# A graph network with experts: twelve-head outputs kept in SBUF in place, and a fourth block in ten formed by VectorE from two broadcast rows

## The chip, the core and the metric

The kernel runs on one core of a Trainium2 chip. The metric is the device time of one execution in microseconds (us). The runs of the kernel before gave 3488.45, 3494.69 and 3496.25 us.

## What is computed

Four blocks, each with a residual, over 1250 nodes with 768 features: a three-layer graph attention network (heads 12 x 64, 12 x 64, 1 x 768) on 20,000 edges; a mixture of 8 experts, top 2; a two-layer graph attention network (4 x 512, 1 x 768); a second mixture of experts. The change touches the first two attention layers, called layers 0 and 1 below, and the border behind each. One such layer:

```python
def _gat_layer(x, W, attn_l, attn_r, bias, src, dst, num_heads, head_dim, use_elu):
    z = (x @ W).reshape(N, num_heads, head_dim)
    el = jnp.sum(z * attn_l, axis=-1)
    er = jnp.sum(z * attn_r, axis=-1)
    e = jax.nn.leaky_relu(el[src] + er[dst], NEG_SLOPE)      # slope 0.2
    m = jax.ops.segment_max(e, dst, num_segments=N)
    ex = jnp.exp(e - m[dst])
    denom = jax.ops.segment_sum(ex, dst, num_segments=N)
    alpha = ex / denom[dst]
    msg = alpha[:, :, None] * z[src]
    out = jax.ops.segment_sum(msg, dst, num_segments=N)
    out = out + z + bias.reshape(1, num_heads, head_dim)
    if use_elu:
        out = jax.nn.elu(out)
```

## The kernel before

**Dense attention.** The graph is turned once into a dense table of edge counts, source by destination, in SBUF. Nodes are cut into T = 10 tiles of P = 125. A head works on 20 blocks j: two halves of the destinations (HALF = 625 columns) times ten tiles s of sources. A block holds the weights of 125 sources for 625 destinations.

**One block.** With r1 = er - m and r2 = 0.2 er - m per destination, and el per source, the exponent is 0.2 el + max(0.8 el + r1, r2), which is also 0.2 el + relu(0.8 el + 0.8 er) + r2. In layers 0 and 1 the kernel uses the second form:

- ScalarE writes the rectified block, relu(0.8 er + 0.8 el), into `r2[half][:, s % 3]` (`relu`, L1309), three blocks ahead, from a broadcast row of er (`erb`). It does this for all 20 blocks.
- Adding r2, in one of two ways. For most blocks TensorE multiplies by `spread`, an identity with a row of ones below; the row of r2 lies in partition 125 of the same buffer (`exponents`, L1020, two products per block). For the tiles in `ADD_AT` = [3, 7, 9], 6 of the 20 blocks, VectorE adds a broadcast row `rb2` (`add_r2`, L1758) three blocks ahead.
- ScalarE takes the exponential (L1322); VectorE limits it and multiplies by the edge counts into the weights (`weights`, L1681).
- TensorE multiplies the weights of the other half, one half behind, with z and a column of ones (`sum_tile`, L1030). Each j does five sources of one destination tile; the second j of a half waits for all ten weightings of the half before.

**Around the blocks.** Every second j VectorE takes one tile of the masked maximum for the head after next (`max_tile`, L1614), ten in a head (in head 0: 20; in the last two: none); it needs the broadcast row of that head's el (`elb`). `max_end` then makes r1 and r2 of ten tiles as columns; TensorE transposes them at j = 11 (`turn_r`), ScalarE copies them at j = 12 (L1292), and SyncE spreads them through DRAM.

**SyncE's order** in a head (`lay_r2`, L604 to L616): store the row of r2 (L604), wait for it, load `rb2` broadcast over 125 partitions (L610), load three copies of the short row for the first half into partition 125 (L616), load the next but one head's `elb` (L595), then, when TensorE is through with the head before, the short rows of the second half; then `erb` (L598). A broadcast load reads 1250 numbers of 4 bytes into each of 125 partitions.

**The end of a head.** `finish` divides the sums of a half by their denominators and adds z, on VectorE (L1695 to L1702); GpSimd stores each half to the DRAM tensor `raw` (L768). At j = 1 and 11 of the next head.

**The border between layers** (`gat_to_gat`). When the first half of the last head is summed, SyncE asks for the next layer's weights (L550). It then waits for all stores (`previous_stored`), asks for the three vectors al, ar and bias (L555, L557) and loads the ten input tiles (L584), each once the product of the tile two before has started (`x_free`). VectorE adds the bias and forms elu with ScalarE (`prep`, L1537 to L1541); TensorE transposes the tile (L909) and multiplies it with the weights (L919); ScalarE copies z (L1237); VectorE takes el and er of it (`score`, L1562, L1564, in layer 2 L1552). VectorE's order is prep(t + 2), score(t).

## Time and profile before

| what | value |
|---|---|
| runs | 3488.45, 3494.69, 3496.25 us |
| profiled execution, its own time | 3496.23 us |
| its span | 3494.5 us |
| TensorE busy | 2914.8 us, 83% |
| VectorE busy | 1911.9 us, 55% |
| ScalarE busy | 1137.0 us, 33% |
| GpSimd busy | 212.1 us, 6% |
| mean granted TensorE clock | 0.911 of full |

The profile names TensorE PE (its weight loads PEld), VectorE DVE, ScalarE ACT, GpSimd POOL and SyncE's queue SPq; "arena" is the one SBUF buffer that most tiles are cut from. Busy shares are means over stages with different limits. Layers 0 and 1 with their borders lie between about 350 and 1610 us of the span.

### The profile page before, as it was taken

The page shows a single profiled execution, that of the slowest core. Times are in us where ns is not written, and L with a number is a line of the kernel's source. Part 1 is how long each engine was busy: PE and PEld are TensorE (multiplying, and loading weights), DVE is VectorE, ACT ScalarE, POOL GpSimd, SP SyncE. Part 2 cuts the span into 40 slices and gives each one's busy share as a digit, 9 for nine tenths or more (in the row PEclk, how much of TensorE's full clock was granted, in tenths as well). Part 3 has the DMA queues.
Part 4 walks back from the last instruction along what each step waited for, and adds up shares of the span by engine and source line. Part 5 has one row for each costly group of instructions (what it writes and reads, how often), then busy time and mean ns, then how long its engine had stood idle before and what let it go on. Part 6 is the DMA issues. An engine that isn't in the chain of part 4 may idle for free.

```text
span 3494.5 us, 45857 instructions
## 1 busy us (share of the span) xinstructions
PE 2914.8 (83%) x14613; PEld 2141.8 (61%) x14614; DVE 1911.9 (55%) x3661; ACT 1137.0 (33%) x1827; POOL 212.1 (6%) x237
## 2 busy tenths in 40 slices
PE   6875799996849999966978849979996898896984
PEld 4543688885438888833656624458885555465762
DVE  7755899983579999536541124476640334532113
ACT  1121688873237877612103301121110211211110
POOL 0000000000000000100001120000000000000112
PEclk9988899998969999988988979979998999897995
DMA  1011121112012111110124642112213110023434
GB/s 66 0 36 47 45 69 54 56 49 62 31 58 60 55 57 62 47 49 25 44 72 153 197 147 83 48 70 73 82 37 126 46 47 17 33 76 113 167 135 137
DMA packets 90489, 246.94 MB, mean 71 GB/s; under 512 B 19129, under 2 KB 31875, under 8 KB 87497
## 3 DMA queue, kind: packets, MB, share of 16 engines
q1 hardware_dynamic: 60761, 174.51, 13.9%
q0 software_dynamic: 23216, 55.62, 6.4%
q10 hardware_dynamic: 6400, 15.36, 1.3%
q8 instruction: 65, 1.06, 0.1%
q14 instruction: 47, 0.39, 0.0%
HBM read 185.28 MB, written 62.62 MB: 71 GB/s over the span
## 4 chain that ended last, share of the span: by engine, by line
PE 38%; DVE 6%; DMA 5%; issue 2%; ACT 1%; SPq 0%; POOL 0%; ACTq 0%; DVEq 0%; POOLq 0%
PE psum L1000 17%; PE psum L919 10%; PE psum L1125 4%; PE psum L1134 4%; DMA arena<-y_rows,arena 1%; DVE arena L1552 1%; DMA y_rows<-arena 1%; DMA arena<-xn_rows,arena 1%; PE psum L1073 1%; DVE arena L1851 1%; DMA arena<-raw 1%; DVE arena L1670 1%; PE psum L1107 1%; PE psum L1112 1%; PE psum L909 0%
## 5 line engine op out<-in xcount | busy, mean ns | idle before, releaser
L919 PE MATMUL psum<-arena 128*125 128x384 f32 (+1 forms) x1840 | 666.7, 522 | 7.3 <-ACT arena L1237 7.3
L1000 PE MATMUL psum<-arena 125*125 125x256 f32 (+3 forms) x2400 | 631.4, 423 | 46.0 <-DVE arena L1684 46.0
L1030 PEld LDWEIGHTS psum<-arena 125*125 125x125 f32 x4800 | 578.8, 190 | 70.2 <-DVE arena L1681 15.8
L1000 PEld LDWEIGHTS psum<-arena 125*125 125x125 f32 x2400 | 450.7, 190 | 215.6 <-DVE arena L1684 39.9
L1030 PE MATMUL psum<-arena 125*125 (+1 forms) x4800 | 566.8, 271 | 15.5 <-DVE arena L1681 15.5
L919 PEld LDWEIGHTS psum<-arena 128*125 128x125 f32 x1840 | 347.1, 191 | 300.5 <-issue 118.6
L1020 PE MATMUL psum<-arena,spread 126*125 126x313 f32 (+1 forms) x1344 | 438.3, 450 | 31.7 <-DMA arena<-r_rows 18.7
L1681 DVE SCALAR_TENSOR_TENSOR arena<-arena,edge_counts 125x625 f32<-125x625 f32 x480 | 381.3, 804 | 75.9 <-ACT arena L1322 75.8
L1614 DVE CUSTOM_DVE_ANT_0 arena<-arena,no_edge_bias 125x1250 bf16<-125x1250 f32 x270 | 392.5, 1454 | 43.4 <-DMA arena<-el_rows 40.6
L1309 ACT ACTIVATE arena<-arena,el 125x625 f32<-125x625 f32 x480 | 386.4, 806 | 38.3 <-DMA arena<-el_rows 38.3
L1322 ACT ACTIVATE arena<-psum,el 125x625 f32<-125x625 f32 x336 | 262.4, 781 | 198.9 <-PE psum L1020 175.8
L1020 PEld LDWEIGHTS psum<-arena,spread 126*125 126x125 f32 x1344 | 232.4, 193 | 93.6 <-DMA arena<-r_rows 18.7
L1958 DVE COPY arena<-psum 128x384 f32<-128x384 f32 x47 | 26.2, 557 | 377.8 <-PE psum L1134 349.6
L909 PE MATMUL psum<-ident,arena 125*128 125x125 f32 x400 | 63.1, 303 | 203.1 <-DVE arena L1541 123.4
L1300 ACT ACTIVATE arena<-arena,el 125x625 f32<-125x625 f32 x120 | 97.4, 817 | 293.3 <-DVE arena L1670 293.3
L909 PEld LDWEIGHTS psum<-ident,arena 125*128 125x128 f32 x400 | 49.1, 155 | 228.8 <-DVE arena L1541 103.9
L1552 DVE CUSTOM_DVE_ANT_0 arena<-arena 125x512 bf16<-125x512 f32 (+1 forms) x120 | 93.7, 781 | 170.2 <-ACT arena L1237 156.9
L1125 PEld LDWEIGHTS psum<-arena 128*128 128x128 f32 x1416 | 172.5, 200 | 21.1 <-issue 12.5
L1125 PE MATMUL psum<-arena 128*128 128x128 f32 x1416 | 175.6, 285 | 11.6 <-issue 9.4
L1134 PE MATMUL psum<-arena 128*128 128x384 f32 x472 | 164.2, 496 | 14.2 <-ACT arena L1400 13.7
L1209 ACT ACTIVATE arena<-arena 125x768 f32<-125x768 f32 (+1 forms) x30 | 35.9, 1198 | 415.2 <-DVE arena L1539 415.2
L768 POOL DMA_DIRECT2D raw<-arena x48 | 78.7, 1640 | 1394.1 <-DVE arena L1702 1293.5
(209 smaller groups left out, 2454.8 us busy)
## 6 DMA issues: line engine op xcount, KB each, us to landing
arena<-el_rows SPq DMA_DIRECT2D x51, 610.4 KB
arena<-in_L_ffn_W SPq DMA_DIRECT2D x16, 1152.0 KB, 8.8
y_rows<-arena SPq DMA_DIRECT2D x47, 384.0 KB, 2.4
arena<-r_rows SPq DMA_DIRECT2D x24, 610.4 KB
arena<-in_L_w SPq DMA_DIRECT2D x16, 768.0 KB, 6.3
arena<-in_L_gnn_W SPq DMA_DIRECT2D x4, 3072.0 KB, 14.7
raw<-arena POOLq DMA_DIRECT2D x40, 250.0 KB, 2.8
arena<-raw SPq DMA_DIRECT2D x10, 1000.0 KB
```

The source lines that it names most:

```text
L909: ins = e.transpose(banks[g % 2][:, k * P:(k + 1) * P], L.xin[u][:, (k0 + k) * 128:(k0 + k + 1) * 128], ident[0:P, 0:P])
L919: ins = e.matmul(bank[0:P, 0:w], L.xt[u][:, k, :], L.w_sb[:, k, at:at + w], start=(k == 0), stop=(k == L.KT - 1))
L1000: ins = e.matmul(banks[2 + 2 * (j % 2) + c][0:P, 0:w], Ph[half][:, s, d * P:(d + 1) * P], (L.zh[u] if L.spill else L.z)[:, s, at:at + w], ...
L1020: ins = e.matmul(o[:, at:to], spread[:, :], L.r2[half][:, s % 3, at:to], start=True, stop=True)
L1030: ins = e.matmul(banks[2 + half][0:P, d * 65:(d + 1) * 65], Ph[half][:, s, d * P:(d + 1) * P], L.z[:, s, h, :], start=(s == 0), stop=(s == ...
L1125: ins = e.matmul(banks[6][:, ci * ST:(ci + 1) * ST], M.w1s[u][:, k, ci * 128:(ci + 1) * 128], M.xgt[:, k, :], start=(k == 0), stop=(k == C ...
L1134: ins = e.matmul(banks[2 + c][:, 0:C // 2], M.ht[:, ci, :], M.w2s[u][:, ci, c * (C // 2):(c + 1) * (C // 2)], start=(ci == 0), stop=(ci == ...
L1309: e.activation(L.r2[half][0:P, s % 3, :], L.erb[u][:, half * HALF:(half + 1) * HALF], ACT.Relu, bias=L.el8[:, s, bass.ds(h, 1)], scale=1.0 ...
L1322: e.activation(L.ex[j % 4], src, ACT.Exp, bias=L.el2[:, s, bass.ds(h, 1)]).then_inc(L.e_ready, 1)
L1552: ins = e.tensor_tensor_reduce(L.sjunk[:, 0:L.D], zt, L.al_b[r][:, h, :], 1.0, 0.0, ALU.mult, ALU.add, L.elr[:, t, r * L.H + h:r * L.H + h ...
L1614: st.add(e.tensor_tensor_reduce(L.junk, L.elb[u], MB[:, t, :], 1.0, -3.0e38, ALU.add, ALU.max, mx[:, t:t + 1]))
L1681: e.scalar_tensor_tensor(out=Ph[half][:, s, :], in0=L.ex[j % 4], scalar=2.0, in1=counts, op0=ALU.min, op1=ALU.mult).then_inc(L.p_ready, 1)
```

## The change

- The outputs of layers 0 and 1 are not stored. `finish` keeps each half's quotient in `og`, and at the second half VectorE adds both halves to z in place (the first half no longer gets an addition of its own). GpSimd's stores and the waits for them fall away.
- The next layer's `prep` reads its input tile from z in SBUF. Its vectors lie where `elb` was, and SyncE asks for them right behind the weights; the input loads fall away. VectorE waits for `x_free` itself. In layer 2 the ones beside z are written after the last prep.
- `ADD_AT` is [3, 5, 7, 9]: 8 of 20 blocks. VectorE forms such a block whole, max(r1 + 0.8 el, r2), from two broadcast rows, `rb1` and `rb2`, and ScalarE makes no rectified block for it. TensorE makes the other 12.
- SyncE stores both rows, and loads `rb1` ahead of `rb2`, in the same queue.

```diff
@@ -40,13 +40,18 @@
-ADD_AT = [3, 7, 9]
+ADD_AT = [3, 5, 7, 9]
 ADDS, TURNS = 2 * len(ADD_AT), 2 * (T - len(ADD_AT))
 def of_vector(j):
     return sum(v % T in ADD_AT for v in range(j))
+
+
+def rectified(j):
+
+    return j - of_vector(j)
 def split(total, parts):
...
@@ -87,6 +92,7 @@
     def __init__(self, name, heads, width, k_tiles, prep, spill, add_z, signals, before):
...
@@ -252,6 +258,8 @@
         Z_AT, Z_W = P_AT + P_W, 10260
         S_AT = Z_AT + Z_W
         Z_END = Z_AT + T * (C + 1)
+        ROWS_FROM = Z_AT + T * 12 * 65
+        HEADS_AT = ROWS_FROM + 2 * N
...
@@ -338,9 +346,9 @@
+            L.src = [A["x"], None, None, None, raw3][n]
             L.src_bias = [None, A["L0_gnn_b0"], A["L0_gnn_b1"], None, A["L1_gnn_b1"]][n]
-            L.dst = raw[n]
+            L.dst = raw3
             L.w_sb = carve(P_AT, 128, L.KT * L.F).rearrange("p (k f) -> p k f", k=L.KT)
...
@@ -348,12 +356,14 @@
             else:
+                if L.inner is not None:
+                    at = HEADS_AT + 2 * N
                 L.xin = [carve(at + u * L.K, P, L.K) for u in range(2)]
                 at += 2 * L.K
             if L.prep == "elu":
                 L.low = [carve(at + u * L.K, P, L.K) for u in range(2)]
                 at += 2 * L.K
-                L.xbias = carve(at, P, L.K)
+                L.xbias = carve(HEADS_AT + 2 * L.F if L.inner is not None else at, P, L.K)
                 at += L.K
             L.xt = [carve(at + u * L.KT * P, 128, L.KT * P).rearrange("p (k n) -> p k n", k=L.KT) for u in range(2)]
...
@@ -362,10 +372,10 @@
-            vectors_at = MADE_AT if L.spill else S_AT - 2 * L.F
+            vectors_at = MADE_AT if L.spill else HEADS_AT if L.inner is not None else S_AT - 2 * L.F
             L.al_b = [carve(vectors_at + u * L.F, P, L.F).rearrange("p (h d) -> p h d", h=L.H) for u in range(2)]
-            at = S_AT
+            at = HEADS_AT if L.batched else S_AT
             if L.H > 1:
                 L.elb = [carve(at + u * N, P, N) for u in range(2)]
...
@@ -380,6 +390,7 @@
                 at += 4 * HALF
                 L.rb2 = [carve(at + u * N, P, N) for u in range(2)]
                 at += 2 * N
+                L.rb1 = [carve(ROWS_FROM + u * N, P, N) for u in range(2)]
             else:
                 L.rb = [carve(at + u * 2 * N, P, 2 * N).rearrange("p (r d) -> p r d", r=2) for u in range(min(2, L.H))]
...
@@ -577,6 +588,7 @@
         def gat_sync(e, L):
             if not L.spill:
                 load_vectors(e, L)
+            if not L.spill and L.inner is None:
                 with e.Fori(0, HT) as i:
...
@@ -601,13 +613,14 @@
                 e.wait_ge(L.rt_sb, L.since["rt_sb"] + h + 1)
                 apart(e)
-                e.dma_start(r_rows[h, T:2 * T, :], L.rt[u][T:2 * T, :]).then_inc(L.r_out[u], 16)
+                e.dma_start(r_rows[h, :, :], L.rt[u]).then_inc(L.r_out[u], 16)
                 e.wait_ge(L.r_out[u], L.since["r_out"][u] + 16 * (i + 1))
                 apart(e)
                 if not isinstance(i, int) or i > 0:
                     e.wait_ge(L.added, L.since["added"] + ADDS * (h - 1))
                     apart(e)
-                e.dma_start(L.rb2[u], over(r_rows[h, T:2 * T, :].rearrange("t p -> (t p)"))).then_inc(L.rb2_in[u], 16)
+                for rows, r in ((L.rb1, 0), (L.rb2, 1)):
+                    e.dma_start(rows[u], over(r_rows[h, r * T:(r + 1) * T, :].rearrange("t p -> (t p)"))).then_inc(L.rb2_in[u], 16)
                 for half in range(2):
                     if not first:
                         e.wait_ge(L.t_ready, L.since["t_ready"] + TURNS * (h - 1) + TURNS // 2 * (half + 1))
...
@@ -640,7 +653,7 @@
                 def rows_of(h, u, i, more):
-                    e.wait_ge(L.relued, L.since["relued"] + 2 * T * (h - 1))
+                    e.wait_ge(L.relued, L.since["relued"] + TURNS * (h - 1))
...
@@ -739,7 +752,8 @@
             if following.KT * following.F > T * HALF:
                 p_is_free(e, L)
             load_projection(e, following, 1)
-            previous_stored(e, L)
+            if following.inner is None:
+                previous_stored(e, L)
...
@@ -763,18 +777,13 @@
         def gat_gpsimd(e, L):
             def store(h):
                 for half in range(2):
-                    if L.batched:
-                        e.wait_ge(L.out_done, L.since["out_done"] + 2 + 2 * h + half + 1)
-                        e.dma_start(by_tile(L.dst)[:, half * HT:(half + 1) * HT, bass.ds(h * 64, 64)],
-                                    L.og[half][:, 0:HT * 64].rearrange("p (t f) -> p t f", t=HT)).then_inc(L.stored[half], 16)
-                        continue
                     for d in range(HT):
                         j = half * HT + d
                         e.wait_ge(L.out_done, L.since["out_done"] + 2 + T * h + j + 1)
                         e.dma_start(by_tile(L.dst)[:, j, bass.ds(h * L.D, L.D)],
                                     L.og[j % 2][:, 0:L.D]).then_inc(L.stored[j % 2], 16)
-            if L.H > 1:
+            if L.spill:
                 with e.Fori(0, L.H) as h:
                     store(h)
...
@@ -1013,7 +1022,7 @@
                 half, s = j // T, j % T
                 if s == 0:
                     e.wait_ge(L.r2_in[half], L.since["r2_in"][half] + 48 * (h + 1))
-                e.wait_ge(L.relued, L.since["relued"] + 2 * T * h + j + 1)
+                e.wait_ge(L.relued, L.since["relued"] + TURNS * h + rectified(j) + 1)
                 e.wait_ge(L.e_ready, L.since["e_ready"] + 2 * T * h + j + 1)
...
@@ -1302,6 +1311,8 @@
             def relu(h, u, i, j):
                 half, s = j // T, j % T
+                if s in ADD_AT:
+                    return
                 if j == 0:
...
@@ -1515,7 +1526,7 @@
         def gat_vector(e, st, L):
             e.wait_ge(L.v_in, L.since["v_in"] + L.vectors)
-            if not L.spill:
+            if L.batched or L.inner is None and not L.spill:
                 e.memset(L.z_ones, 1.0).then_inc(L.ones, 1)
...
@@ -1527,8 +1538,17 @@
                     e.wait_ge(L.x_free, L.since["x_free"] + t + 1)
                     norm_b(e, st, L.xin[u], x, u, L.mid, L.since["mid"] + t + 1, L.prepped)
                     return
+                x = L.xin[u]
+                if L.inner is not None:
+                    e.wait_ge(L.x_free, L.since["x_free"] + t + 1)
+                    by_head = lambda a: a.rearrange("p (h d) -> p h d", d=64)
+                    st.add(e.tensor_tensor(by_head(x), L.inner.z[:, t, :, 0:64], by_head(L.xbias), ALU.add))
+                    st.wait()
+                    e.tensor_scalar(L.low[u], x, 0.0, None, ALU.min).then_inc(L.half_prep, 1)
+                    e.wait_ge(L.mid, L.since["mid"] + t + 1)
+                    e.scalar_tensor_tensor(out=x, in0=L.low[u], scalar=-1.0, in1=x, op0=ALU.add, op1=ALU.max).then_inc(L.prepped, 1)
+                    return
                 e.wait_ge(L.x_in[u], L.since["x_in"][u] + 16 * (i + 1))
-                x = L.xin[u]
                 if L.prep == "ln":
...
@@ -1567,6 +1587,8 @@
                 ins.then_inc(L.scored, 1)
                 e.wait_ge(L.scored, L.since["scored"] + 2 + t + 1)
+            if L.inner is not None:
+                st.wait()
             prep(0, 0, 0)
...
@@ -1595,6 +1617,8 @@
                                                   ALU.add, ALU.max, part[g][:, t:t + 1]))
             if not L.batched:
+                if L.inner is not None:
+                    e.memset(L.z_ones, 1.0).then_inc(L.ones, 1)
                 max_part(0, range(T))
             score(T - 2, 0)
...
@@ -1684,10 +1708,11 @@
                 e.scalar_tensor_tensor(out=Ph[half][:, s, :], in0=L.e[j % 2], scalar=2.0,
                                        in1=counts, op0=ALU.min, op1=ALU.mult).then_inc(L.p_ready, 1)
-            rd = small[0:P, 110:110 + HT]
+            rds = [small[0:P, 110 + half * HT:110 + (half + 1) * HT] for half in range(2)]
             def finish(h, half, tiles=range(HT)):
+                rd = rds[half if L.batched else 0]
                 if L.batched:
                     e.wait_ge(L.ag_ready, L.since["ag_ready"] + 2 * h + half + 1)
                     sums = banks[2 + half][0:P, 0:HT * 65].rearrange("p (t f) -> p t f", t=HT)
...
@@ -1696,10 +1721,14 @@
                     st.wait()
                     st.add(e.reciprocal(rd, rd))
                     st.wait()
-                    e.wait_ge(L.stored[half], L.since["stored"][half] + 16 * h)
-                    st.add(e.tensor_tensor(o, sums[:, :, 0:64], rd.rearrange("p (t o) -> p t o", o=1).to_broadcast([P, HT, 64]), ALU.mult))
-                    st.wait()
-                    e.tensor_tensor(o, o, L.z[:, half * HT:(half + 1) * HT, h, 0:64], ALU.add).then_inc(L.out_done, 1)
+                    e.tensor_tensor(o, sums[:, :, 0:64], rd.rearrange("p (t o) -> p t o", o=1).to_broadcast([P, HT, 64]),
+                                    ALU.mult).then_inc(L.out_done, 1)
+                    if half == 0:
+                        return
+                    e.wait_ge(L.out_done, L.since["out_done"] + 2 + 2 * h + 2)
+                    for part in range(2):
+                        zh = L.z[:, part * HT:(part + 1) * HT, h, 0:64]
+                        st.add(e.tensor_tensor(zh, L.og[part][:, 0:HT * 64].rearrange("p (t f) -> p t f", t=HT), zh, ALU.add))
                     return
                 for d in tiles:
                     j = half * HT + d
...
@@ -1751,11 +1780,12 @@
                 half, s = j // T, j % T
                 if j == ADD_AT[0]:
-                    e.wait_ge(L.rb2_in[u], L.since["rb2_in"][u] + 16 * (i + 1))
-                e.wait_ge(L.relued, L.since["relued"] + 2 * T * h + j + 1)
+                    e.wait_ge(L.rb2_in[u], L.since["rb2_in"][u] + 32 * (i + 1))
                 e.wait_ge(L.p_ready, L.since["p_ready"] + 2 * T * h + j + 1)
                 apart(e)
-                e.tensor_tensor(L.ex[j % 4], L.r2[half][0:P, s % 3, :], L.rb2[u][:, half * HALF:(half + 1) * HALF], ALU.add).then_inc(L.added, 1)
+                cols = slice(half * HALF, (half + 1) * HALF)
+                e.scalar_tensor_tensor(out=L.ex[j % 4], in0=L.rb1[u][:, cols], scalar=L.el8[:, s, bass.ds(h, 1)], in1=L.rb2[u][:, cols],
+                                       op0=ALU.add, op1=ALU.max).then_inc(L.added, 1)
             def batched_head(h, u, i, first, more):
```

## Rows read from the trace of the kernel before

**Rows 1.** Table of stretches, busy us (instructions) of each engine, TensorE's mean granted clock, DMA share, GB/s.

```profile
408.60:816.30 407.70, 406.36 (x2851) 356.88 (x2852) 367.62 (x600) 323.51 (x447) 36.14 (x22) 1.00 0.18 52
...
827.70:851.80 24.10, 0.00 (x0) 0.00 (x0) 1.41 (x6) 0.00 (x0) 1.64 (x1) 0.56 0.25 75
851.80:961.20 109.40, 91.33 (x300) 53.42 (x300) 58.61 (x66) 24.66 (x49) 0.00 (x0) 0.93 0.09 31
...
1476.70:1500.40 23.70, 0.07 (x2) 0.00 (x0) 1.39 (x5) 0.00 (x0) 1.64 (x1) 0.55 0.26 76
```

**Rows 2.** Timeline, TensorE's weight loads of three products: start us, us, line, operation.

```profile
621.48 0.83 PEld L1020 LDWEIGHTS psum<-arena,spread 126*125 126x125 f32 x4
...
623.63 0.83 PEld L1020 LDWEIGHTS psum<-arena,spread 126*125 126x125 f32 x4
...
626.87 0.83 PEld L1020 LDWEIGHTS psum<-arena,spread 126*125 126x125 f32 x4
```

**Rows 3.** Timeline of the same head, all engines; in brackets idle time and its releaser.

```profile
596.90 1.46 DVE L1614 CUSTOM_DVE_ANT_0 arena<-arena,no_edge_bias 125x1250 bf16<-125x1250 f32 x1 [1.46 <-DMA arena<-el_rows]
...
613.30 1.52 DVE L1681 SCALAR_TENSOR_TENSOR arena<-arena,edge_counts 125x625 f32<-125x625 f32 x2
...
614.74 1.45 DVE L1614 CUSTOM_DVE_ANT_0 arena<-arena,no_edge_bias 125x1250 bf16<-125x1250 f32 x1
...
614.96 1.30 PE L1030 MATMUL psum<-arena 125*125 x10 [0.49 <-DVE arena L1681]
...
618.28 0.25 ACT L1292 ACTIVATE arena<-psum 20x125 f32<-20x125 f32 x1
...
620.25 0.28 SPq L610 DMA_DIRECT2D arena<-r_rows  x1
...
633.35 1.46 DVE L1614 CUSTOM_DVE_ANT_0 arena<-arena,no_edge_bias 125x1250 bf16<-125x1250 f32 x1
```

**Rows 4.** Groups by line and form: busy us, mean ns | idle before, releasers.

```profile
L1670 DVE SCALAR_TENSOR_TENSOR arena<-arena,el 125x625 f32<-125x625 f32 x120 | 103.0, 863 | 0.2
...
L1702 DVE TENSOR_TENSOR arena<-arena 125x320 f32<-125x320 f32 x48 | 23.6, 493 | 5.6 <-DVE arena L1700 4.4
```

**Rows 5.** Waits of VectorE, 400 to 820 us: us in total, times, longest.

```profile
DVE arena L1614 <- DMA arena<-el_rows: 7.7, 6, 2.4
```

**Rows 6.** Timeline of layer 1, third head.

```profile
1080.59 0.29 SPq L610 DMA_DIRECT2D arena<-r_rows  x1
...
1096.30 1.46 DVE L1614 CUSTOM_DVE_ANT_0 arena<-arena,no_edge_bias 125x1250 bf16<-125x1250 f32 x1 [4.10 <-DMA arena<-el_rows]
```

**Rows 7.** Table of two stretches, columns as in rows 1.

```profile
626.50:636.50 10.00, 10.00 (x71) 8.68 (x71) 9.79 (x19) 7.67 (x12) 0.00 (x0) 1.00 0.32 128
817.50:824.50 7.00, 7.00 (x66) 7.00 (x66) 0.51 (x2) 0.00 (x0) 1.64 (x1) 1.00 0.99 345
```

**Rows 8.** Timeline of the border between layers 0 and 1.

```profile
836.28 0.29 SPq L555 DMA_DIRECT2D arena<-in_L_gnn_al  x1
...
848.88 0.16 DVE L1519 MEMSET arena<- 125x120 f32 x1 [19.86 <-DMA arena<-in_L_gnn_b]
851.76 0.96 DVE L1537 TENSOR_TENSOR arena<-arena 125x768 f32<-125x768 f32 x1 [2.73 <-DMA arena<-raw]
```

**Rows 9.** Timeline of layer 0's first head.

```profile
349.46 0.27 SPq L610 DMA_DIRECT2D arena<-r_rows  x1
...
356.91 4.53 PE L1020 MATMUL psum<-arena,spread 126*125 126x313 f32 x8 [9.10 <-DMA arena<-r_rows]
```

**Rows 10.** Timeline of layer 1's input tiles.

```profile
909.93 0.96 DVE L1537 TENSOR_TENSOR arena<-arena 125x768 f32<-125x768 f32 x1 [2.94 <-DMA arena<-raw]
...
913.49 0.86 PE L909 MATMUL psum<-ident,arena 125*128 125x125 f32 x6 [1.83 <-DVE arena L1541]
...
914.18 7.91 PE L919 MATMUL psum<-arena 128*125 128x384 f32 x24
...
945.54 15.65 PE L919 MATMUL psum<-arena 128*125 128x384 f32 x48
```

More of the change, by code:

```diff
@@ L89, in __init__ @@
     def __init__(self, name, heads, width, k_tiles, prep, spill, add_z, signals, before):
+        self.inner = before if before is not None and before.batched else None
         self.name, self.H, self.D, self.KT = name, heads, width, k_tiles
@@ L115, in __init__ @@
         self.totals = dict(
[L116 removed]
+            w_in=[16] * 2, v_in=self.vectors, scored=T, x_in=[16 * HT * (not spill and self.inner is None)] * 2, x_free=T, half_prep=T, mid=T, prepped=T, tp_ready=G * T, xt_ready=G * T,
             zp_ready=NC * T, z_ready=NC * T, ones=1, spilled=[16 * HT * spill] * 2, elt_ready=3 * told, elt_sb=3 * told, scaled=1, el_out=16 * told,
```

10 lines of the change are left out of this document (4 added, 6 removed).

## The prediction

> **What bounds the kernel now.** I read the granted clock and the page first, then a table of stretches, then the timeline of one twelve-head layer, because the change lives in layers 0 and 1 and at the two borders behind them. The heads of layer 0 from the second on take 407.7 us [rows 1]; TensorE is busy for 406.36 us of that and VectorE for 367.62 us, at full clock. TensorE takes 2.15 us for a plain block (621.48 to 623.63) and 3.24 us for a plain one and one of VectorE's (623.63 to 626.87) [rows 2], so 1.1 us for the latter: 14 x 2.14 + 6 x 1.10 = 36.6 us a head, some 37.1 with the transpose and the two signalling products. Eleven heads of that are the 407.7 us: TensorE sets the pace of every head. But VectorE is close behind. From one head's first maximum to its eleventh it takes 17.84 us (596.90 to 614.74), and from there to the next head's first 18.61 us (614.74 to 633.35) [rows 3]: 36.45 us of work without a gap in a head of 37.1 us. At 614.96 TensorE already waits 0.49 us for VectorE [rows 3]. So 0.7 us per head is all the room there is.
>
> At the borders nobody works: from 827.7 to 851.8 us and from 1476.7 to 1500.4 us TensorE is idle and its mean granted clock is 0.56 and 0.55, mostly the lower level of 1.2 GHz [rows 1]. The heads' sums go to DRAM, SyncE then asks for three vectors at 836.28, they are in at 848.88 and the first input tile at 851.76 [rows 8]. The ten input tiles then take 109.4 us [rows 1].
>
> **The change, part by part.**
>
> *TensorE per head.* One more block in each half does without its two spread products. By [rows 2] a half falls by 2.14 - 1.10 = 1.04 us and a head to 35.0 us. That is worth something only where TensorE still sets the pace: in the last two heads of each layer, which have no maxima.
>
> *VectorE per head.* Instructions start 0.72 us apart (two weightings in 1.52 us, each 0.80) [rows 3]. Two more additions: +1.44. All eight are now of the form of L1670, 863 ns [rows 4], where I take the old addition to last as long as a weighting, 0.80; +0.06 each, +0.48. Its scalar is picked by a register, for which no row of VectorE has a price; it can be computed while the instruction before runs, so I take 0, and as the upper end the same 0.06 us again, +0.5 a head. In finish the first half loses L1702 (493 ns, about 0.1 of it overlapped) and the wait before it, -0.65; the second has one more, +0.42, and a drain before the next maximum, +0.10. Sum: 36.45 + 1.44 + 0.48 - 0.13 = 38.24 us. VectorE becomes the bound: +1.1 us a head, TensorE's 35.0 being under it. The part from the eleventh maximum to the next head's first grows from 18.61 to 18.61 + 0.72 + 0.24 + 0.52 = 20.1 us.
>
> *The queue that the added row is put into.* This is the step I trust most to matter. In lay_r2 SyncE now issues rb1 (625,000 bytes) ahead of rb2, the three short rows and load_el. load_el brings the row that the next head's first maximum reads. It is late already: VectorE waits for el_rows 6 times in layer 0's heads, 7.7 us in all [rows 5]; so far the 0.7 us per head and TensorE's pace hide that. The order of events [rows 3]: weighting 9, the second of the pair at 613.30, ends at 614.82, TensorE's sum waits for it and starts at 614.96, then comes the transpose, ScalarE copies the row at 618.28, and the DMA of rb2 is issued at 620.25, 5.51 us behind the eleventh maximum. The row of maxima landed 15.71 us behind that issue in the worst head I found (1080.59 to 1096.30) [rows 6], 13.1 or less where there was no wait (620.25 to 633.35 [rows 3]); with 13.1 + 1.3 in the six that wait and less in the others I take 13.8. These broadcast loads come one after another at 128 GB/s with 0.32 of the sixteen engines busy, while a weight load moves 345 GB/s at 0.99 [rows 7]; one more is 625,000 / 128,000 = 4.9 us. With the stores to DRAM gone I take 0.5 off: landing at 13.8 + 4.9 - 0.5 = 18.2 us behind the issue, 5.5 + 18.2 = 23.7 us behind the eleventh maximum, where VectorE wants it at 20.1. It stands for 3.6 us with nothing else to do (everything behind the maximum is in its order), and because TensorE's sum, the transpose and the DMA hang on weighting 9, nothing is caught up: 38.24 + 3.6 = 41.8 us a head, +4.7. This holds where a head's first maximum reads a row that was fetched in the head before while VectorE is the bound: heads 2 to 9, 16 in both layers: +75 us. Bounds of the wait: 12.7 (the head at 620.25, a little under its 13.1) + 4.9 - 0.5, less 5.5 to 20.1, gives 2.5 us; 14.2, midway to the worst head, with 5.1 for the row gives 4.7 us; +57 to +93 us.
>
> That the speed is that of few engines is the row's 0.32. The Trainium skill (SBUF — State Buffer, "The DMA setup-cost knee") fits a transfer as 2 us plus bytes over 436,000 per us, which would be 1.4 us for the added row, a wait of 0.2 us and a faster kernel; the trace says 4.9. The Trainium skill (DMA: Bandwidth & Descriptors, "Why a DMA increments its semaphore by 16 and not by 1") has the reason: a transfer gets the largest number of engines up to 16 that divides its slowest dimension, for 125 partitions 5; the 0.32 agrees (5 of 16 is 0.31).
>
> *The rest of each layer.* The first head's first product waits for the short rows behind rb2 (TensorE's start at 356.91 is put down to r_rows [rows 9]): +4.9. Head 0, bound by VectorE, has no finish saving: +1.9. Head 1: +1.1, its row came early. Last two heads: -2.1 each, but the rows of head 11 now land some 16.8 us behind the transpose, where TensorE wants them at 13.1: +3.7, so -0.5. Together +7.4 a layer, +14.8.
>
> *The borders.* Nothing waits for a store. The vectors are issued right behind the two weight loads, whose traffic ends about 825 [rows 7]; from their issue the three took 12.6 us before (836.28 to 848.88), about 1.2 of it, by my estimate, ahead of the first byte, so they are in at about 825 + 11.4 = 836.4. The last finish is done at 830 and hides under that. The first input tile needs no load: L1537 starts at 836.4 instead of 851.76: -15.4, and the same at the other border. Bounds: -12 if the vectors come as late as 840, -21.5 if they come ahead of the finish at 830. The vectors load into the maxima's rows, which are free by then.
>
> *The ten tiles.* A tile takes 10.45 us now (914.18 to 945.54 is three), because L1537 waits for a tile's load that was asked for when the product of two tiles before started [rows 10]. After: TensorE's 7.74 us (48 products in 15.65, 24 in 7.91) + 0.86 of transposes [rows 10] = 8.6; VectorE, busy 58.61 us for ten tiles [rows 1], fits under it. Of the nine intervals the first is at the lower clock and stays, and the last is back to back already. The other seven gain 1.85 by the steady tile; but ten tiles in 109.4 us leave them 10.7 on average, the earlier ones being longer, so I take 2.1: -14.7 a layer, bounds -10 and -17. Both borders and both sets of tiles: -30.8 - 29.4 = -60.
>
> *Sum:* +75 + 14.8 - 60 = +29 or so. The profiled execution took 3496.23 us with a span of 3494.5, the runs' median is 3494.69; I put the forecast at the median's level, 3523 us, **0.8% slower**. With the bounds of the wait (+57, +93) and of the borders and tiles (-52, -68) it is +4 to +55: 3499 to 3549.
>
> **The rivals.**
>
> *The added row comes for free, and the kernel is faster.* If rb1 runs beside rb2, or at the weight load's 345 GB/s (1.8 us), the maxima's row lands at 5.5 + 13.8 + 0 to 1.8 = 19.3 to 21.1 us against 20.1: no wait up to 1.0 us. A head then costs 1.1 to 2.1 us, 18 to 34 for sixteen; the rest of the layers about -2 to +2; the borders -60: -44 to -24, 3450 to 3470 us. The sign turns where the added row costs about 3.1 us instead of 4.9 (29 over 16 is 1.8 less). For it: VectorE's measured waits average only 1.3 us (7.7 over 6) [rows 5], and the stores' traffic goes. Against: rb2, the el row and the er row run back to back at one speed, never side by side [rows 7]. 18%. The skill's fit above belongs here.
>
> *TensorE stays the bound and takes its 2.1 us a head.* -50 for 24 heads on top of the borders, about 3390 us. It needs VectorE to shed 3 us a head; [rows 3] have it without a gap. 2%.
>
> *The queue hurts more.* If the landing scatters like the 15.7 us case, or the late rows stop TensorE too, the wait is 6 us: +38 more, 3560 us. 8%.
>
> The forecast has 72%. Most of it is above 3502 us; a tenth of the total chance lies within 0.2% (7 us, about what a measurement of this kernel can tell), where wait and borders meet at their favourable ends. Range 3466 to 3550: it leaves out the deepest part of the first rival and most of the last. Faster 0.20, same 0.10, slower 0.70.
>
> **What would show it.** VectorE's L1614 waiting for el_rows some 3.6 us in heads 2 to 9, about 55 to 60 us in sum, and almost nothing of it in head 1; TensorE's half-heads 20 us or more apart instead of 18.6; TensorE idle on L1681; the last two heads near 35 us each; the first L1537 of layer 1 about 7 us behind the last finish; tiles 8.6 us apart. If L1614's waits stay under 1 us a head, the queue step is wrong and the kernel is faster. If the first L1537 still waits for vectors past 840, the border is mis-sized.

## The result and the profile after

Slower: 3588.88 us, median of 4 runs (3582.75 to 3601.51), against 3494.23 (3488.45 to 3496.25) for the kernel before on the same chip; ratio 1.0278, 95% interval 1.0245 to 1.0312. The direction was forecast; the size, +94.6 us, is three times the +29 and above the range. The profiled run took 3583.82 us, its span 3582.1 at a mean granted clock of 0.883; before 0.911, over a span of 3494.5.

The table of stretches answers [rows 1]: busy us (instructions) of PE, PEld, DVE, ACT, POOL, then TensorE's granted clock, DMA share, GB/s. Heads are counted from 0, as in the code. The first row is the eleven heads of layer 0 behind head 0, the second and third are heads 2 to 9 of layers 0 and 1; then come the two halves of head 3, and the border between layers 0 and 1 with its ten tiles.

```profile
404.65:889.65 485.00, 440.49 (x2783) 384.74 (x2782) 398.34 (x639) 266.94 (x365) 0.00 (x0) 0.87 0.14 52
...
446.73:807.95 361.22, 328.18 (x2026) 286.14 (x2026) 305.07 (x491) 197.38 (x270) 0.00 (x0) 0.85 0.15 57
1138.16:1495.87 357.71, 325.88 (x2026) 284.04 (x2025) 302.40 (x488) 190.76 (x264) 0.00 (x0) 0.87 0.15 57
...
491.52:524.22 32.70, 28.80 (x127) 24.59 (x126) 21.75 (x37) 12.18 (x17) 0.00 (x0) 0.63 0.12 49
524.22:541.79 17.57, 17.57 (x129) 15.64 (x129) 16.48 (x27) 11.79 (x17) 0.00 (x0) 1.00 0.15 52
900.90:907.50 6.60, 0.12 (x2) 0.01 (x2) 1.74 (x5) 0.00 (x0) 0.00 (x0) 0.77 0.28 111
907.50:1006.00 98.50, 87.78 (x300) 52.14 (x300) 61.92 (x70) 25.63 (x50) 0.00 (x0) 0.95 0.00 0
```

Heads 2 to 9 now take 44.9 us each on average (718.9 over the sixteen of both layers); forecast were 41.8. Before they took 37.5 (599.9 over sixteen), counted between the same signals of TensorE:

```profile
442.53:741.98 299.45, 298.18 (x2089) 261.43 (x2089) 285.83 (x471) 240.46 (x333) 26.22 (x16) 1.00 0.20 59
1090.58:1391.04 300.46, 298.46 (x2090) 261.31 (x2089) 284.56 (x471) 235.85 (x329) 26.22 (x16) 1.00 0.20 59
```

TensorE is no longer at full clock: 0.87 over the eleven heads against 1.00. And the loss is not spread over a head: the second half of head 3 goes in 17.57 us at clock 1.00, TensorE busy throughout, the first half in 32.70 at 0.63. The border, on the other hand, fell from 24.10 to 6.6 us and its tiles from 109.40 to 98.50 [rows 1].

What happens in the first half, from the timelines of TensorE, SyncE's queue and VectorE (start us, us, engine, line; idle time and its releaser in brackets). They answer to [rows 2, 3].

```profile
482.60 0.80 SPq L623 DMA_DIRECT2D arena<-r_rows  x2
483.63 0.92 SPq L629 DMA_DIRECT2D arena<-r_rows  x3
484.74 0.28 SPq L607 DMA_DIRECT2D arena<-el_rows  x1
...
488.19 1.27 PE L1029 MATMUL psum<-arena,spread 126*125 126x313 f32 x4
489.30 2.29 PE L1039 MATMUL psum<-arena 125*125 x20
491.52 0.19 PE L1043 MATMUL psum<-ident 128*1 128x1 f32 x2
495.60 2.44 PE L1029 MATMUL psum<-arena,spread 126*125 126x313 f32 x4 [3.90 <-DMA arena<-r_rows]
...
506.21 4.31 PE L1039 MATMUL psum<-arena 125*125 x20
...
516.59 2.33 PE L1029 MATMUL psum<-arena,spread 126*125 126x313 f32 x4
518.76 2.29 PE L1039 MATMUL psum<-arena 125*125 x20
...
500.34 1.46 DVE L1638 CUSTOM_DVE_ANT_0 arena<-arena,no_edge_bias 125x1250 bf16<-125x1250 f32 x1 [4.36 <-DMA arena<-el_rows]
...
507.47 0.81 DVE L1705 SCALAR_TENSOR_TENSOR arena<-arena,edge_counts 125x625 f32<-125x625 f32 x1 [1.18 <-ACT arena L1333]
...
513.75 0.81 DVE L1705 SCALAR_TENSOR_TENSOR arena<-arena,edge_counts 125x625 f32<-125x625 f32 x1 [2.60 <-ACT arena L1333]
```

Read it in this order. rb1 and rb2 are issued at 482.60, the short rows at 483.63 behind them in one queue. The short rows land at 495.60, 13.0 us after the first issue; the head began at 491.52. TensorE stands 3.90 us, and its first four spread products then take 2.44 us instead of 1.27, twenty sum products 4.31 instead of 2.29: the granted clock is at the lower of its two levels, 1.2 GHz, until past 516, although TensorE works without a gap from 495.60 on. The el row lands 17.7 us behind the issue and VectorE stands 4.36 us; but from 507 on VectorE stands again, 1.18 and 2.60 us, now behind ScalarE, which waits for TensorE's slow products.

Waits in the eleven heads (us in total, times, longest), the last row, VectorE's for the el row, to be held against [rows 5]:

```profile
ACT arena L1333 <- PE psum L1029: 138.8, 89, 5.1
DVE arena L1705 <- ACT arena L1333: 46.6, 40, 5.4
PE psum L1029 <- DMA arena<-r_rows: 43.9, 11, 5.7
...
DVE arena L1638 <- DMA arena<-el_rows: 33.7, 9, 5.0
```

The border between layers 0 and 1 in VectorE's timeline, against [rows 8]:

```profile
900.94 0.16 DVE L1720 TENSOR_SCALAR small<-psum 125x5 f32<-125x5 f32 x1 [10.06 <-PE psum L1039]
...
907.55 0.95 DVE L1545 TENSOR_TENSOR arena<-arena 125x768 f32<-125x768 f32 x1 [4.77 <-issue]
```

The group of the added operation (busy us, mean ns | idle before), against [rows 4]:

```profile
L1787 DVE SCALAR_TENSOR_TENSOR arena<-arena,el 125x625 f32<-125x625 f32 x192 | 166.1, 865 | 0.0
```

### The profile page after: what moved, and what is told of

The parts are those of the page before. It is cut to its first block, busy times and chain, and to the rows that moved or that the text cites. A ratio compares the mean times of both kernels' runs of the same rounds, so it can differ in the third digit from the quotient of the medians.

```text
span 3582.1 us, 44936 instructions
## 1 busy us (share of the span) xinstructions
PE 2976.5 (83%) x14421; PEld 2198.7 (61%) x14422; DVE 1959.3 (55%) x3709; ACT 1004.2 (28%) x1635; POOL 132.8 (4%) x189
## 4 chain that ended last, share of the span: by engine, by line
PE 37%; DVE 6%; DMA 5%; issue 2%; ACT 1%; SPq 0%; POOL 0%; ACTq 0%; DVEq 0%; POOLq 0%
PE psum L1009 17%; PE psum L928 10%; PE psum L1134 4%; PE psum L1143 4%; DMA arena<-y_rows,arena 1%; DVE arena L1572 1%; DMA y_rows<-arena 1%; DMA arena<-xn_rows,arena 1%; PE psum L1082 1%; DVE arena L1881 1%; DMA arena<-raw 1%; DVE arena L1694 1%; PE psum L1116 0%; PE psum L1121 0%; PE psum L918 0%
## 5 line engine op out<-in xcount | busy, mean ns | idle before, releaser
L1039 PEld LDWEIGHTS psum<-arena 125*125 125x125 f32 x4800 | 637.9, 208 | 67.5 <-issue 27.1
L1039 PE MATMUL psum<-arena 125*125 (+1 forms) x4800 | 620.2, 288 | 8.0 <-DVE arena L1705 8.0
L1009 PEld LDWEIGHTS psum<-arena 125*125 125x125 f32 x2400 | 449.7, 189 | 215.6 <-DVE arena L1708 40.0
L1333 ACT ACTIVATE arena<-psum,el 125x625 f32<-125x625 f32 x288 | 224.5, 780 | 401.3 <-PE psum L1029 350.6
L1787 DVE SCALAR_TENSOR_TENSOR arena<-arena,el 125x625 f32<-125x625 f32 x192 | 166.1, 865 | 0.0
```

Of the source, the lines that this page charges most:

```text
L1009: ins = e.matmul(banks[2 + 2 * (j % 2) + c][0:P, 0:w], Ph[half][:, s, d * P:(d + 1) * P], (L.zh[u] if L.spill else L.z)[:, s, at:at + w], ...
L1039: ins = e.matmul(banks[2 + half][0:P, d * 65:(d + 1) * 65], Ph[half][:, s, d * P:(d + 1) * P], L.z[:, s, h, :], start=(s == 0), stop=(s == ...
L1333: e.activation(L.ex[j % 4], src, ACT.Exp, bias=L.el2[:, s, bass.ds(h, 1)]).then_inc(L.e_ready, 1)
L1787: e.scalar_tensor_tensor(out=L.ex[j % 4], in0=L.rb1[u][:, cols], scalar=L.el8[:, s, bass.ds(h, 1)], in1=L.rb2[u][:, cols], op0=ALU.add, op ...
```

## The experiments

Theories: **A**, the short rows, late behind the added row, stop TensorE at each head's start, and its clock falls behind the stop. **B**, the step on record: the late el row sets VectorE's pace. **C**, VectorE's own added work. Each kernel was run beside the kernel before, whose median was 3496.89, 3496.92 and 3498.36 us in the three groups of four.

### Order and clock

**r2_first.** In lay_r2 the load of rb1 and rb2 moves into the loop, behind the short rows of half 0.

```
 for half in range(2):
     ... three short rows ...
+    if half == 0:
+        for rows, r in ((L.rb1, 0), (L.rb2, 1)): e.dma_start(rows[u], ...)
     if half == 0 and more:
         load_el(h + 2, u)
```

> The changed kernel with the first three short rows of a head (L629, half 0) issued ahead of the two broadcast rows instead of behind them; the el row stays last. Theory A (the short rows are late, TensorE stands about 4 us at each head's start, its granted clock falls to half behind it, and this is what the forecast missed): the pause of L1029 falls to what it was before (under 1 us), the clock rises from 0.88 to 0.92 or more, the VectorE wait for the el row stays at 4 to 6 us a head, so heads go at about 41.8 us as forecast on record: 3515 to 3540 us. Theory B (only the late el row sets the pace, the short rows wait beside it): no gain, 3580 to 3595. Theory C (VectorE's own work with eight blocks is dearer than thought): no gain, 3580 to 3595.

3534.51 us, ratio 1.0099 (1.0064 to 1.0133): 54 us better than the change and in A's range, but partly by luck. A had the heads at 41.8 us and the clock at 0.92 or more; heads 2 to 9 take 44.3 us (709.2 over sixteen, against 718.9 in the change) and the clock is 0.893. Of the 48 us between the two profiled executions only some 10 come from these sixteen heads and 29 from heads 10 and 11 of both layers, which go back to 74.3 us a pair. TensorE's stop moved and did not go: VectorE stands 39.6 us in heads 2 to 9 of layer 0 for the el row, up to 7.9 at a time, and then TensorE stands behind ScalarE and VectorE and drops all the same (first heads 2 to 9 of layer 0, then VectorE's and TensorE's timeline):

```profile
442.48:798.32 355.84, 323.74 (x2025) 280.41 (x2025) 302.34 (x489) 195.53 (x269) 0.00 (x0) 0.88 0.15 58
...
454.26 1.46 DVE L1639 CUSTOM_DVE_ANT_0 arena<-arena,no_edge_bias 125x1250 bf16<-125x1250 f32 x1 [6.12 <-DMA arena<-el_rows]
...
459.73 2.45 PE L1030 MATMUL psum<-arena,spread 126*125 126x313 f32 x4 [3.67 <-ACT arena L1334]
```

**el_first.** load_el is issued ahead of rb1 and rb2, the short rows stay last.

```
+if more: load_el(h + 2, u)
 for rows, r in ((L.rb1, 0), (L.rb2, 1)): ...
```

> The changed kernel with the el row (L607) issued ahead of the two broadcast rows; the short rows stay behind them and so land about 4.9 us later than in the changed kernel. Theory A (TensorE's pause for the short rows and the clock behind it): VectorE's wait for the el row vanishes, the pause of L1029 grows from 4 to 8 or 9 us a head, and the kernel gets slower: 3620 to 3680 us. Theory B (the el row sets the pace): 3500 to 3520, faster than the changed kernel by 70 or more. Theory C: no change within 10 us of 3588.

3726.43 us (3700.23 to 3745.27), ratio 1.0624 (1.0556 to 1.0693). B falls as the main cause: with the el row in time (VectorE has no wait for it left between 446 and 800 us) the kernel is 138 us slower still, and what is later is the short rows. A had the sign and not the size (3620 to 3680). At the seven head starts between 446 and 800 us TensorE stands 62.3 us in all:

```profile
PE psum L1029 <- DMA arena<-r_rows: 62.3, 7, 10.4
```

**warm.** Nothing is loaded earlier; TensorE works while it waits.

```
 if s == 0:
+    if half == 0:
+        for _ in range(16):
+            e.matmul(banks[1][0:128, 0:128], ident, ident)
     e.wait_ge(L.r2_in[half], ...)
```

> The changed kernel with 16 matmuls of 128x128 of the identity (output unused, in bank 1) on TensorE ahead of each head's wait for the short rows, so that TensorE works through the most of its pause of 3.5 to 4.4 us; nothing is loaded earlier. Theory A (the clock behind the pause is a good part of the loss): granted clock 0.95 or more in the heads, gain of 2 to 3 us a head, 3525 to 3555 us. Theory B and C (the clock is a companion, VectorE or its row sets the pace anyway): within 8 us of 3588, or slower where the pause was shorter than the 16 matmuls.

3499.76 us (3493.79 to 3505.69, 10 runs), ratio 0.9999 (0.9984 to 1.0015): 89 us less than the change, by work that nobody uses, and 25 us below the range that A gave. Its stretches, heads 2 to 9 of both layers:

```profile
447.46:779.68 332.22, 316.47 (x2281) 279.56 (x2280) 301.59 (x489) 195.10 (x269) 0.00 (x0) 1.00 0.16 61
1103.31:1433.62 330.31, 316.28 (x2282) 279.58 (x2281) 301.58 (x489) 190.00 (x265) 0.00 (x0) 1.00 0.16 62
```

TensorE's timeline at one head's start, and VectorE's waits in heads 2 to 9 of layer 0:

```profile
489.18 3.84 PE L1026 MATMUL psum<-ident 128*128 128x128 f32 x32
494.74 1.31 PE L1032 MATMUL psum<-arena,spread 126*125 126x313 f32 x4 [1.73 <-DMA arena<-r_rows]
```
```profile
DVE arena L1641 <- DMA arena<-el_rows: 25.5, 8, 4.5
```

The short rows are as late as ever (494.74 is 13.0 us behind the issue of rb1 at 481.70), the clock is 1.00, and a head takes 41.4 us (662.5 over sixteen). That is the forecast's head: VectorE busy 301.59 / 8 = 37.7 (forecast 38.24) and a wait for the el row of 25.5 / 8 = 3.2 us (forecast 3.6). So the clock is the loss that the forecast missed in these heads, and the queue step is right where the clock holds. The two runs mirror each other: in r2_first the short rows are in time and the clock falls, and a head takes 44.3 us; in warm they are late and the clock holds, and it takes 41.4. The Trainium skill (TensorE: Matmul & The Clock Gate, "HAM oscillation — how this bites in real kernels") tells of a matmul kernel that waits for a DMA ahead of each tile and starts every tile at half clock; the trace after agrees, at 495.60 and in every head behind head 0: all 22 first halves have a mean granted clock below 1 (0.57 to 0.93), all second halves 1.00.

**before_rb1.** The kernel before, with rb1 stored, loaded ahead of rb2 and read by nobody (the layout gives it the room that it has in the changed kernel).

```
-e.dma_start(L.rb2[u], over(r_rows[h, T:2 * T, :]...))
+for rows, r in ((L.rb1, 0), (L.rb2, 1)):
+    e.dma_start(rows[u], over(r_rows[h, r * T:(r + 1) * T, :]...))
```

> The kernel before with one thing added: the slope-1 rows too are stored, and loaded as broadcast row rb1 ahead of rb2 (L623 of the changed kernel), and nobody reads them. Stores, reloads and the six rectified blocks stay. Theory A (the place of the load in the queue, by way of the short rows and the clock): slower than before by 60 to 90 us, 3555 to 3585, with the pause of L1029 at each head and a clock near 0.88. Theory B (the queue, but by the el row alone; VectorE has 1.8 us a head less work here than in the changed kernel): slower by 40 to 60, 3535 to 3555. Theory C (VectorE's added blocks, not the queue): within 10 us of 3494.

3682.61 us, ratio 1.0522 (1.0466 to 1.0578): one unread 625,000-byte load a head costs 186 us, more than twice what I expected. The signs are those of the change: TensorE stands for the short rows (26.9 us in heads 2 to 9 of layer 0) and its next products are at the lower level. VectorE's waits for the el row are longer too, 55.2 us in the same heads against 33.1 in the change, so this run does not price the two late rows apart. Why it costs more than the change was not shown; that TensorE has 37.1 us of work a head here instead of 35.0, a part of it at the lower level, is my reading. The same four products take 1.27 us at full clock (488.19 in the change):

```profile
453.63 2.42 PE L1024 MATMUL psum<-arena,spread 126*125 126x313 f32 x4 [3.05 <-DMA arena<-r_rows]
455.84 2.21 PE L1034 MATMUL psum<-arena 125*125 x10
```

C is out as the main cause: VectorE's work here is that of before.

### The halves, and the loads in time

**inplace_only.** The changed kernel with the old blocks.

```
-ADD_AT = [3, 5, 7, 9]
+ADD_AT = [3, 7, 9]
 ... relu for every block, rb1 not loaded ...
-e.scalar_tensor_tensor(out=L.ex[j % 4], in0=L.rb1[u]..., in1=L.rb2[u]..., op0=ALU.add, op1=ALU.max)
+e.tensor_tensor(L.ex[j % 4], L.r2[half][0:P, s % 3, :], L.rb2[u]..., ALU.add)
```

> Half of the change alone: outputs in place in SBUF, no stores and reloads, the new layout; blocks stay as in the kernel before (three places a half, rectified block plus rb2, one broadcast row a head). The step on the borders as on record: 14.7 + 15.4 a layer twice, so 3494 - 60 = about 3434 us (3420 to 3445), with heads at 37 to 38 us and no pause at their starts. If the in-place sums lengthen the heads (a rival), 3450 to 3475.

3422.40 us (3414.37 to 3425.07), ratio 0.9780 (0.9759 to 0.9800): -74.5 us. Heads 2 to 9 of layer 0 take 37.19 us each and TensorE is busy without a gap:

```profile
441.16:738.65 297.49, 297.49 (x2089) 261.70 (x2088) 287.01 (x473) 240.12 (x333) 0.00 (x0) 1.00 0.13 50
```

**tworow_only.** The kernel before with the blocks from two rows, at four places a half; stores and reloads stay.

```
-ADD_AT = [3, 7, 9]
+ADD_AT = [3, 5, 7, 9]
 ... rb1 and the new add_r2 as in the change; store() and the x_in loads as before ...
```

> The other half alone: four places a half formed from two broadcast rows, stores and reloads kept. If the halves add up (the queue, the late short rows and the clock all belong to this half): 3588 + 60 = about 3650 us (3630 to 3665), with the pause of L1029 and a clock near 0.88 as in the changed kernel. If the loss needed both halves (a rival: the in-place sums or the layout delay the heads): 3500 to 3590.

3673.38 us (3653.77 to 3688.65), ratio 1.0483 (1.0448 to 1.0518): +176.5, somewhat over what was expected. With -74.5 the halves give +102, the whole +94.6: they add up, about. before_rb1 and this one lie 9 us apart, so what is computed from rb1 hardly matters in sum beside its being loaded where it is; VectorE's added work and TensorE's saved work, which pull opposite ways, are both in that difference.

**both_first.** Short rows, el row, then rb1 and rb2.

```
 if half == 0 and more: load_el(h + 2, u)
+if half == 0:
+    for rows, r in ((L.rb1, 0), (L.rb2, 1)): ...
```

> The changed kernel with the order short rows, el row, rb1, rb2. The broadcast rows then land about 17.7 us behind the first issue, where VectorE wants them about 10 to 11 us behind it (first added block, just behind the start of the head). Theory A (any stand of TensorE of 3 us or more halves the clock, whichever load is last): VectorE waits 5 to 7 us for rb2 instead of the el row, TensorE stands behind it: 3520 to 3570 us, clock 0.90 or less. Theory B (only the el row counts): 3450 to 3480.

3523.88 us (3510.61 to 3540.03), ratio 1.0080 (1.0047 to 1.0113), clock 0.894, as A said: in these three orders (r2_first, el_first, this one) somebody waits for the load that comes last. Now it is VectorE's first added block, between 446 and 800 us:

```profile
DVE arena L1788 <- DMA arena<-r_rows: 24.7, 8, 5.7
```

**split_both.** As both_first, every broadcast row in two loads.

```
+PARTS = [(0, 112), (112, 125)]
-e.dma_start(rows[u], over(r_rows...))
+for a, b in PARTS:
+    e.dma_start(rows[u][a:b, :], over(r_rows..., b - a))
 (load_el likewise)
```

> As both_first, and each broadcast load of a head (el, rb1, rb2) is issued in two parts, partitions 0 to 111 and 112 to 124, so that more DMA engines than five share it. Theory A: the three rows land within 6 to 9 us of the first issue, no engine stands at a head's start, clock 0.95 or more, VectorE's own 38.2 us a head is what is left: 3440 to 3470 us. If the part of the loss is VectorE's own work rather than the loads: 3500 or more. If more engines do not shorten a load: as both_first.

3467.22 us (3462.56 to 3471.24), ratio 0.9911 (0.9893 to 0.9930). The loads stop being a matter: in heads 2 to 9 of layer 0 no wait for them is left, and while they run the DMA moves 260 GB/s at a share of 0.87, where the change has 120 at 0.32, the level of [rows 7]. A stretch of the change and then stretches of split_both (loads running; heads 2 to 9; the two halves of head 4):

```profile
484.00:494.00 10.00, 7.71 (x61) 6.93 (x59) 10.00 (x15) 6.84 (x9) 0.00 (x0) 1.00 0.32 120
```
```profile
515.50:520.50 5.00, 5.00 (x39) 4.47 (x37) 5.00 (x8) 3.07 (x5) 0.00 (x0) 1.00 0.87 260
...
445.27:762.22 316.95, 301.26 (x2025) 262.73 (x2025) 301.67 (x489) 195.54 (x269) 0.00 (x0) 0.95 0.22 65
...
521.64:550.01 28.37, 26.13 (x127) 22.45 (x127) 22.93 (x38) 14.23 (x20) 0.00 (x0) 0.70 0.09 30
550.01:567.57 17.56, 17.56 (x128) 15.63 (x127) 16.47 (x27) 11.79 (x17) 0.00 (x0) 1.00 0.39 102
```

A head takes 39.6 us, where VectorE is busy for 301.67 / 8 = 37.7. TensorE's timeline in the first half of head 4:

```profile
527.62 2.35 PE L1046 MATMUL psum<-arena 125*125 x10 [2.21 <-DVE arena L1712]
529.77 2.39 PE L1036 MATMUL psum<-arena,spread 126*125 126x313 f32 x4
```

The Trainium skill (DMA: Bandwidth & Descriptors, "Why a DMA increments its semaphore by 16 and not by 1") gives the rule, the largest number up to 16 that divides the slowest dimension: all sixteen engines for 112 partitions and five for 125. The traces agree, with 0.87 and 0.32 of the sixteen engines busy. Yet the clock is 0.900, where A expected 0.95 or more, so its time (3440 to 3470) came out without its reason. TensorE, with 35.0 us a head, runs ahead of VectorE until it has no block to sum, stands 2.21 us in one piece, and is at half clock again. Of heads 2 to 9 of layer 0, two pay it in full (4 and 7, first halves of 28.4 and 26.7 us) and one a little (2, 21.7 us); the others have stands too and keep the clock.

### Three or four blocks, and the version to keep

**split_warm.** split_both with the filler of warm.

```
+for _ in range(16): e.matmul(banks[1][0:128, 0:128], ident, ident)   (half 0, ahead of the wait for r2_in)
```

> split_both (short rows, el row, then the broadcast rows, each broadcast load in two parts) with the 16 identity matmuls at the start of each head. In split_both the loads were in time, but TensorE, 3 us a head quicker than VectorE, still ran ahead until it stood some 2.2 us, and each such stand was followed by a half at half clock. Theory A (only that lump of idle time costs more than VectorE's own pace): clock 1.0 in the heads, every head at VectorE's 37 to 38.3 us: 3425 to 3445 us. Rival (slow halves come from a wait of VectorE for something else): 3460 to 3480, as split_both.

3445.13 us, ratio 0.9850 (0.9822 to 0.9877), at the upper edge of the expected range. From head 2 on all heads take 38.65 us at clock 1.00 (21.09 and 17.56 us a half) and TensorE has no idle time in them: the fillers, 3.5 us a head, are in its way now.

**three.** The change with three places a half and nothing else.

```
-ADD_AT = [3, 5, 7, 9]
+ADD_AT = [3, 7, 9]
```

> The changed kernel with three places a half instead of four (ADD_AT 3, 7, 9), still formed from two broadcast rows, order of loads and outputs as changed. If the queue and the clock are the loss, this recovers nothing: the short rows are as late, and TensorE has 2 us a head more to do, at half clock for a part of it 4: 3590 to 3640 us. If VectorE's fourth pair of blocks is the loss: 3430 to 3500.

3567.25 us (3561.89 to 3591.79), ratio 1.0213 (1.0163 to 1.0264): going back to three places gives some 21 us of the 94.6, and the intervals of the two ratios overlap a little. Both expectations missed: the queue's side had no gain or a loss (3590 to 3640), C 3430 to 3500, which is farther off. Beside inplace_only the three-place form with its added row costs 145 us.

**split_three.** split_both with the same edit as *three*.

> split_both with three places a half. TensorE has 37.1 us a head, VectorE 38.24 - 2 x 0.865 = 36.5: TensorE is the later one again, so it does not run ahead, does not stand, and keeps its clock: 3415 to 3430 us, as inplace_only (3422). If the two-row form or the split loads cost anything by themselves: 3440 or more.

3413.15 us (3409.39 to 3427.40), ratio 0.9750 (0.9723 to 0.9778), 2 us under the expected range: the lowest median, though its interval overlaps that of inplace_only.

```profile
410.00:800.00 390.00, 390.00 (x2739) 343.03 (x2737) 357.72 (x579) 268.81 (x371) 0.00 (x0) 1.00 0.21 60
```

TensorE has no idle time in 390 us. *three* has the same two-row blocks and costs 145 us more than inplace_only; here they cost nothing that can be seen, so those 145 us belong to how and when the rows are loaded.

**inplace_old4.** inplace_only with a fourth place a half: one row a head, the queue of before.

```
-ADD_AT = [3, 7, 9]
+ADD_AT = [3, 5, 7, 9]
```

> inplace_only with four places a half in the old form (rectified block plus rb2, 493 ns), one broadcast row a head, order of loads as before. TensorE 35.0 us a head, VectorE 36.45 + 2 x 0.49 = 37.4: VectorE sets the pace. Theory A (a TensorE that runs ahead of VectorE stands in lumps and loses its clock): slower than inplace_only though the queue is untouched, 3435 to 3475, clock below 0.91 with single halves of 22 to 28 us. Rival (late rows alone cost): 3420 to 3435, all heads at 37 to 37.5 us.

3485.39 us (3453.17 to 3497.90, 10 runs), ratio 0.9945 (0.9917 to 0.9974): 63 us slower than inplace_only, just above my band, with less work on TensorE and hardly a late load (2.0 us of waits for rows in heads 2 to 9 of layer 0). VectorE is busy for 37.4 us a head, as reckoned, but heads 2 to 9 take 41.8 us in layer 0 and 40.6 in layer 1; the rival had 37 to 37.5. Four of the eight first halves of layer 0 take 26.5 to 31.3 us. One of them:

```profile
493.20:519.67 26.47, 24.41 (x127) 21.00 (x126) 22.55 (x38) 15.41 (x23) 0.00 (x0) 0.74 0.09 37
```

Its start in TensorE's timeline:

```profile
498.86 1.30 PE L1038 MATMUL psum<-arena 125*125 x10 [2.06 <-DVE arena L1702]
500.00 1.88 PE L1028 MATMUL psum<-arena,spread 126*125 126x313 f32 x4
501.68 4.31 PE L1038 MATMUL psum<-arena 125*125 x20
```

## Why the forecast had the sign and missed the size

**What bounds the kernel.** Right: inplace_only and split_three, both with TensorE's 37.1 us a head, keep it busy without a gap; take the work off TensorE and VectorE is the later one (inplace_old4). One reading was off: the 407.7 us [rows 1] start 5.9 us behind the start of head 1. From signal to signal (402.66 to 816.29) the eleven heads take 413.6 us, so a head of before is 37.4 to 37.6 us and not 37.1.

**VectorE per head.** 38.24 forecast, 37.7 busy in warm; the added form is 865 ns, forecast 863, so the scalar that a register picks costs nothing visible. The term was right to about half a microsecond.

**The queue, the step that failed.** It said that the added row makes the el row 4.9 us later (landing 18.2 us behind the issue, measured 17.7), that VectorE then stands 3.6 us in heads 2 to 9, and that a head is 41.8 us. All of that is so at full clock (warm: 37.7, 3.2 and 41.4). What it left out: the three short rows lie behind the same load. The working had this for head 11 (the rows land 16.8 us behind the transpose where TensorE wants them at 13.1, +3.7) and did not ask what it does in the others, since VectorE "sets the pace" there; and it priced TensorE at 35.0 us by rows at clock 1.00, as if that clock came with the engine. Stops of some 4 us were followed by the lower level, for 3.3 us of the first half in the best head (0.93 over 23.35 us) and 31 us in the worst (0.57 over 35.95), and at that level TensorE is the bound again. Sixteen heads: 718.9 us, against 16 x 41.8 = 669: +50. The rival with 8% named the stop of TensorE ("the late rows stop TensorE too") but not the clock, and gave 3560. warm shows that the stop alone would not have cost it.

```profile
541.79:565.14 23.35, 19.17 (x127) 16.72 (x126) 18.59 (x33) 13.26 (x17) 0.00 (x0) 0.93 0.17 70
...
1181.13:1217.08 35.95, 32.07 (x128) 27.39 (x128) 21.95 (x37) 12.34 (x17) 0.00 (x0) 0.57 0.11 45
```

The sign, too, owes something to luck. The forecast had the kernel 29 us slower by the el row's wait alone. With that wait as forecast and the clock held, warm is as fast as the kernel before (0.9999), and its fillers are in that time: what made the change slower is the clock, of which the forecast had nothing.

**The rest of the layer.** Start of the first head +5.3 (360.08 - 347.32, against 7.45 in [rows 9]), forecast +4.9. Heads 10 and 11: forecast -0.5 together; they took 81.70 us in layer 0 and 96.23 in layer 1, where before there were 74.3: +7.4 and +21.9, the same stop and clock. In sum the profiled execution of the change is 87.6 us longer than that of before: heads 2 to 9 give +119.0 (718.9 against 599.9; forecast +75), heads 10 and 11 +29.3 (forecast -1), all the rest -60.7 (forecast -44).

**The borders.** 24.1 and 23.7 us [rows 1] before; after, 6.6 (900.94 to 907.55) and 6.2 (1603.38 to 1609.61): -17.5 each, forecast -15.4; the vectors come sooner. From the first L1537 to the first head's first product: 152.8 us before in layer 1, 143.2 after, the 5.3 above included, so the tiles gave 14.9, forecast 14.7. inplace_only gets -74.5 where the step said -60: by the change's trace 35 are from the borders and, if layer 2's tiles gave what layer 1's did, about 30 from the tiles. Of the ten or so that remain, five are in heads 2 to 9 (595.0 us against 599.9), where VectorE's waits for the el row have become small (2.4 us in layer 0); the rest was not followed.

**The first rival** (the added row free, 3450 to 3470) has split_both, 3467, in its range: with the rows in time the kernel is faster, and the load as written is slow as in [rows 7]. But that run also puts the added row last in the queue, and its heads lose clock (39.6 us against the rival's 38.2 to 39.2), which the rival did not have; the match of the times is in part luck. The second (TensorE takes its 2.1 us a head) needs VectorE to keep up, and none of the runs with four places had that.

What stays open: why like stops cost so differently (first halves of 22.8 to 36.0 us in heads 2 to 9 of the change); no run took that apart. Nor did one take apart why the added load costs 186 us with the stores (before_rb1) and 145 without (*three* against inplace_only).

## What to carry to other kernels

When a transfer is put ahead of others in a queue, list everything behind it with the time at which each is wanted, the small ones first: here the el row in time and the short rows one load later (el_first) cost 138 us more, while the short rows in time and the el row late (r2_first) cost 54 us less. Price a matmul engine's stop by the clock that comes after it and not by its length, and leave the matmul engine a little later than its partner: in-place outputs with three places a half (TensorE 37.1 us a head, VectorE busy for 287.01 / 8 = 35.9 of it) beat four (35.0 and 37.4) by 63 us. If it must wait, idle matmuls can be cheaper than idleness (89 us here), and a broadcast to 125 partitions is better issued as 112 and 13 (57 us from both_first to split_both).

## What the hardware showed unasked

TensorE stood 2.21 us in one piece ahead of 527.62 in split_both, and the products from there on ran at the lower level (ten of the sums in 2.35 us instead of 1.2); in inplace_old4 it stood 2.06 us ahead of 498.86, and the products from about 500 on did. In r2_first a stand of 2.10 us was followed by products at the full level, and in split_both itself one of 2.22 us (third row):

```profile
448.28 1.30 PE L1040 MATMUL psum<-arena 125*125 x10 [2.10 <-DVE arena L1706]
449.42 1.27 PE L1030 MATMUL psum<-arena,spread 126*125 126x313 f32 x4
...
610.47 1.30 PE L1046 MATMUL psum<-arena 125*125 x10 [2.22 <-DVE arena L1712]
```

So the length of a stand alone did not tell, in these rows, whether the clock falls.
